# Attention plus mixture-of-experts layer: ranks product behind the up product of its step, slots of the table of pairs 64 bytes apart

## The reference

```python
x = x + attention(layernorm(x))      # 8 heads of 16, causal, 2048 keys a sequence
xt = layernorm(x)
scores = sigmoid(xt @ gate_w.T)                       # 8 experts
top_scores, top_idx = top_k(scores, 2)
top_scores = top_scores / (sum(top_scores) + 1e-20) * 2.5
h, u = xt @ w1[e], xt @ w3[e]                         # 512 -> 352, for each expert e
routed = sum over the two experts of (silu(h) * u) @ w2[e] * score
shared = silu(xt @ sw1) * (xt @ sw3) @ sw2
x = x + routed + shared
```

## Time and profile before

| | |
|---|---|
| median of 3 runs | 1486.96 us |
| the profiled execution, its own time | 1488.37 us |
| its span, first to last instruction | 1486.5 us |
| mean granted TensorE clock, share of 2.4 GHz | 0.969 |
| PE, DVE, ACT, POOL busy | 93%, 64%, 60%, 30% of the span |

### The profile page before, as it was taken

How to read it: one execution, slowest core, us unless ns; L and a number is a source line. 1 busy time by engine, 2 the same in 40 slices (tenths; PEclk the granted TensorE clock), 3 DMA queues, 4 the chain that set the end, 5 groups by cost and what they waited for, 6 DMA issues and landing times.

```text
span 1486.5 us, 22931 instructions
## 1 busy us (share of the span) xinstructions
PE 1377.3 (93%) x5750; PEld 671.1 (45%) x5751; DVE 951.4 (64%) x2758; ACT 890.7 (60%) x2587; POOL 452.0 (30%) x431
## 2 busy tenths in 40 slices
PE   6997999999999999899899977599999999999996
PEld 4553233333333332355455543255555555555553
DVE  3898998888888874588879885333344444444331
ACT  4663456766666777556555645266666666666663
POOL 0000000000000000000112243677777777777771
PEclk9997899999999999999999998799999999999998
DMA  7775410040050000256577763144444344433442
GB/s 219 231 218 161 109 40 5 24 96 5 9 125 5 1 5 12 84 179 204 144 191 176 211 130 78 45 72 74 74 73 73 71 73 71 73 71 71 71 73 34
DMA packets 124858, 136.83 MB, mean 92 GB/s; under 512 B 37046, under 2 KB 86590, under 8 KB 124774
## 3 DMA queue, kind: packets, MB, share of 16 engines
q1 hardware_dynamic: 101350, 96.56, 24.5%
q0 software_dynamic: 21520, 37.84, 13.8%
q10 hardware_dynamic: 1904, 1.46, 0.4%
HBM read 87.03 MB, written 48.83 MB: 91 GB/s over the span
## 4 chain that ended last, share of the span: by engine, by line
PE 73%; DVE 14%; issue 5%; DMA 4%; ACT 3%; SPq 1%; ACTq 0%; POOL 0%; DVEq 0%; POOLq 0%
PE psum L1052 28%; PE psum L1063 15%; PE psum L975 9%; PE psum L957 7%; PE psum L939 6%; PE psum L889 4%; DVE arena L1242 3%; DVE psum L1240 2%; DMA xn_rows<-xg 1%; DMA attn_cur<-attn_rows 1%; DVE stats L1123 1%; PE psum L960 1%; PE psum L1036 1%; ACT arena L723 1%; PE psum L882 1%
## 5 line engine op out<-in xcount | busy, mean ns | idle before, releaser
L1052 PE MATMUL psum<-arena,xg_t 128*128 (+2 forms) x1648 | 515.5, 466 | 18.9 <-DVE xg_t L1212 18.9
L824 ACT COPY act_t<-act_q 32x96 f32<-32x96 f32 x1648 | 431.8, 262 | 153.2 <-DVE act_q L1333 132.6
L1052 PEld LDWEIGHTS psum<-arena,xg_t 128*128 128x128 f32 x1648 | 315.2, 193 | 220.1 <-issue 63.9
L795 ACT ACTIVATE arena<-psum 128x512 f32<-128x512 f32 (+3 forms) x640 | 303.1, 536 | 172.1 <-PE psum L960 84.6
L657 POOL DMA_INDIRECT table<-const,slot_i x64 | 63.0, 984 | 845.1 <-DVE slot_i L1435 748.6
L673 POOL DMA_INDIRECT xq<-xn_rows,quad_rows x284 | 271.5, 956 | 94.2 <-issue 86.6
L1063 PE MATMUL psum<-arena,act_t 128*128 (+3 forms) x618 | 285.7, 598 | 6.2 <-ACT act_t L824 6.2
L1242 DVE TENSOR_REDUCE arena<-psum 128x1 f32<-128x512 f32 x384 | 251.5, 685 | 41.4 <-PE psum L939 40.8
L939 PE MATMUL psum<-arena 96*128 96x512 bf16 (+3 forms) x640 | 219.5, 363 | 17.2 <-DVE arena L1240 9.2
L957 PE MATMUL psum<-arena 99*128 99x512 bf16 (+3 forms) x640 | 215.0, 353 | 1.6 <-ACT arena L795 0.4
L1323 DVE TENSOR_TENSOR act_sb<-psum,silu 128x352 f32<-128x352 f32 x103 | 53.9, 523 | 238.8 <-ACT silu L847 238.2
(11 more groups left out here) (137 smaller groups left out, 843.3 us busy)
## 6 DMA issues: line engine op xcount, KB each, us to landing
arena<-qk_parts SPq DMA_DIRECT2D x48, 256.0 KB, 6.0
arena<-in_w SPq DMA_DIRECT2D x16, 704.0 KB
arena<-in_x SPq DMA_DIRECT2D x32, 256.0 KB, 4.3
x<-in_x SPq DMA_DIRECT2D x32, 256.0 KB, 3.5
xn_rows<-xg SPq DMA_DIRECT2D x32, 256.0 KB, 2.6
xq<-xn_rows SPq DMA_DIRECT2D x128, 64.0 KB, 2.9
out_rows<-y_sb SPq DMA_DIRECT2D x32, 256.0 KB, 3.3
qk_parts<-arena SPq DMA_DIRECT2D x16, 384.0 KB, 3.2
```

Of the source, the lines that this page charges most:

```text
L795: nc.scalar.activation(probs[:, at_b % PS, d * P:], psum[:, NA + at_b % NBK, 0:CH - d * P], ACT.Exp, scale=float(HD) ** -0.5).then_inc(s_e, 1)
L824: i = nc.scalar.copy(dst, src)
L1052: i = nc.tensor.matmul(psum[:, bank + k % 2, 0:w], xg_t[:, k % 2, c, :], rhs, start=c == 0, stop=c == DC - 1)
```

## The change

- PE: in a step of `COUNT_AT`, `ranks(g)` stands behind `up(n)` instead of at the start of the step. `front(n + 2)` and `turn(n + 3)` go ahead of it, so `ranks` waits for one transposed tile more (`n + 4`) and the wait for `s_cntr` moves to the `turn` of the next step (`n - 4 in COUNT_AT`).
- DVE: `slots(g)` stands behind `turn(n + 1)` of the step instead of at its start.
- The table has 16 words (64 bytes) a slot instead of 2; a put still writes 8 bytes, at slot number times 8 in a view of 8-byte elements, for which `slot_i` is made by a multiplication instead of a copy. The load of a block's pairs takes 256 bytes a partition instead of 32, and the row numbers read every sixteenth word.
- The fill of the table, now 2.16 MB instead of 0.27 MB, moves in SP's queue from the third projection chunk to behind the last load of the second unit's keys and values, in the attention.
- `iota_be` (71 x 8 words a partition) becomes `iota_b` (71 words) and is broadcast over the experts; the constants that are loaded first shrink from 845 to 348 words a partition.

In the diff the first `step` is PE's, the second DVE's.

```diff
+PAIR = 16
...
-               ("quarter", 1), ("own", QP), ("pairs", 2 * TOP_K * NT), ("spare_pairs", 2 * P)):
+               ("quarter", 1), ("own", QP), ("pairs", 2 * TOP_K * NT), ("spare_pairs", PAIR * P)):
...
-        table = dram("table", [TABLE, 2])
+        table = dram("table", [TABLE, PAIR])
...
-                if n == 2:
-                    spare = io["const"][:, CONST["spare_pairs"][0]:CONST["spare_pairs"][1]]
...
                     if n < 2:
                         load_unit(1, (n,))
+                    if n == 1:
+                        spare = io["const"][:, CONST["spare_pairs"][0]:CONST["spare_pairs"][1]]
+                        blocks_of = table.rearrange("(b r) a -> b (r a)", r=P)
+                        for b in range(0, TABLE // P, P):
+                            m = min(P, TABLE // P - b)
+                            sp.dma_start(blocks_of[b:b + m, :], spare[0:m, :]).then_inc(s_table, 16)
...
-                            out=table[:, :], out_offset=bass.IndirectOffsetOnAxis(ap=slot_i[:, q, tt:tt + 1], axis=0),
+                            out=table.rearrange("r (s a) -> (r s) a", a=2), out_offset=bass.IndirectOffsetOnAxis(ap=slot_i[:, q, tt:tt + 1], axis=0),
...
-                    if n - 3 in COUNT_AT:
-                        pe.wait_ge(s_cntr, COUNT_AT[n - 3] + 1)
+                    if n - 4 in COUNT_AT:
+                        pe.wait_ge(s_cntr, COUNT_AT[n - 4] + 1)
...
                 def step(n, k):
-                    if shared and n in COUNT_AT:
-                        ranks(COUNT_AT[n], min(n + 3, NT))
                     if shared and k < count - 2:
                         front(n + 2, k + 2)
                     if shared and k < count - 3:
                         turn(n + 3, k + 3)
                     up(n, k, expert(n))
+                    if shared and n in COUNT_AT:
+                        ranks(COUNT_AT[n], min(n + 4, NT))
                     if k >= 1:
                         down(n - 1, k - 1, expert(n - 1))
...
                 def step(n, k):
-                    if shared and n in COUNT_AT:
-                        slots(COUNT_AT[n])
...
                         if k < count - 1:
                             turn(n + 1, k + 1)
+                        if n in COUNT_AT:
+                            slots(COUNT_AT[n])
...
-                    i = nc.vector.tensor_copy(slot_i[:, q, t0:t0 + m], pick[:, 0:m])
+                    i = nc.vector.tensor_scalar(slot_i[:, q, t0:t0 + m], pick[:, 0:m], float(PAIR // 2), None, ALU.mult)
```

More of the change, by code:

```diff
@@ L48 @@
 QW = P // QP
+PAIR = 16
 CONST = {}
 _at = 0
-for _n, _w in (("ident", P), ("rev8", E), ("first_slot", E), ("iota_be", NB * E),
-               ("quarter", 1), ("own", QP), ("pairs", 2 * TOP_K * NT), ("spare_pairs", 2 * P)):
+for _n, _w in (("ident", P), ("rev8", E), ("first_slot", E), ("iota_b", NB),
+               ("quarter", 1), ("own", QP), ("pairs", 2 * TOP_K * NT), ("spare_pairs", PAIR * P)):
     CONST[_n] = (_at, _at + _w)
@@ L71, in constants @@
     put("first_slot", (np.arange(E) * T)[None])
-    put("iota_be", np.repeat(np.arange(NB), E)[None])
+    put("iota_b", np.arange(NB)[None])
     put("quarter", np.arange(P)[:, None] // QW)
@@ L77, in constants @@
     put("pairs", pairs.reshape(P, -1))
-    spare = np.zeros((P, P, 2), np.float32)
+    spare = np.zeros((P, P, PAIR), np.float32)
     spare[:, :, 0] = T + np.arange(P)[None]
@@ L335, in program @@
         NQ = 4
-        block_quads = sb("block_quads", [P, NQ, 2 * QP])
+        block_quads = sb("block_quads", [P, NQ, PAIR * QP])
         quad_rows = sb("quad_rows", [P, NQ, QP], i32)
@@ L1309, in row_numbers @@
                         dve.wait_ge(ss[f"rows_{k % 2}"], QP * (used(n - NQ, k - NQ) + 16))
-                    quad = block_quads[:, k % NQ, :].rearrange("p (g a) -> p a g", a=2)
+                    quad = block_quads[:, k % NQ, :].rearrange("p (g a) -> p a g", a=PAIR)[:, 0:2, :]
                     own = cf("own").rearrange("p (a g) -> p a g", a=1).broadcast_to([P, 2, QP])
@@ L1449, in block_list @@
                 chain(nc.vector.tensor_tensor_scan(ends, blocks, zero, 0.0, ALU.add, ALU.add))
-                chain(nc.vector.tensor_tensor(by_block, over_b(ends), cf("iota_be").rearrange("p (b e) -> p b e", e=E), ALU.is_le))
+                chain(nc.vector.tensor_tensor(by_block, over_b(ends), cf("iota_b").rearrange("p (b a) -> p b a", a=1).broadcast_to([P, NB, E]), ALU.is_le))
                 chain(nc.vector.tensor_reduce(eid, by_block, AX.X, ALU.add))
@@ L1456, in block_list @@
                 chain(nc.vector.scalar_tensor_tensor(block_slot, eid, float(T // P), start, ALU.mult, ALU.subtract))
-                chain(nc.vector.tensor_tensor(block_slot[0:1, :], block_slot[0:1, :], cf("iota_be")[0:1, :].rearrange("p (b e) -> p b e", e=E)[:, :, 0], ALU.add))
+                chain(nc.vector.tensor_tensor(block_slot[0:1, :], block_slot[0:1, :], cf("iota_b")[0:1, :], ALU.add))
                 chain(nc.vector.tensor_scalar(start_i[:, :], block_slot[0:1, :], float(QW), None, ALU.mult))
```

## The result

| | before | after |
|---|---|---|
| median of the runs, us | 1489.08 (1484.05 to 1494.01, 4 runs) | 1467.3 (1465.11 to 1468.95, 4 runs) |
| the profiled execution: own time, span | 1488.37, 1486.5 | 1468.95, 1467.1 |
| TensorE's mean granted clock | 0.969 | 0.969 |

The ratio is 0.984, with a 95% interval from 0.9814 to 0.9866: faster by 1.6%, forecast 1468.5. (Ratios and intervals here are those on record; they are not the quotients of the medians beside them, from which they differ by up to 0.002.) The total came out as forecast, but not for the reasons given: most of the gain hangs on the spacing, which the forecast had put at 2.4 us.

A forecast was written before the change was run, and what follows sets the result against it. PE was taken as the bound, busy nearly throughout, with DVE nearly as long. Terms -6.5 - 1.1 - 7.8 - 0.7 - 2.4 = -18.5 us, from the median 1486.96, gave 1468.5 us; range for 8 in 10: 1460 to 1481.

The forecast's parts named there:

- Groups 2 to 5 and the seam: Step 27 to first routed product: PE stops waiting for `carry`, group 5's ranks run earlier; -7.8 us (-8.5 to -4.5).
- One sign: Expected in the changed profile: no PE wait for the read of the ranks, and `carry` waits over 0.5 us only at group 5.
- Cured: If spacing stops the clogging: tile 15 in time -1.1, `turn(31)` -1.9, last put -1.0; together -4.0 us.
- Groups 0 and 1: Steps 12 to 15: tile 14 ahead of the puts, -6.5 us (-7.7 to -3); step 20: `front(22)` earlier, -1.1 (-1.6 to 0).
- the walk: Following each group along DVE through the shared expert, counting no PE wait as gained by itself; `up(14)` at 740.9, `up(15)` at 749.3.
- The spacing: Slots 64 bytes apart let row stores land faster beside the puts: -2.4 us, between -4.0 if cured and 0 if not.
- Spacing does nothing: Rival: writes stay 8 bytes, so wider slots change nothing; -16.1 us, 1470.9 us; chance 0.25.
- The store and reload stay the bound: Rival: puts still meet tiles 14, 15 and 29, DVE waits for reloads in PE's place; 1479 us, chance 0.20.
- Slower: wider slots clog more: Rival: wider slots and regions make puts hold up HBM longer, stores over 8 us in the median; 1505 us, chance 0.05.
- Constants, -0.7: Kernel start: smaller constants load sooner, PE's first matmul at 9.6 to 10 us; -0.7 us (-1.0 to 0).
- The fill, 0: Attention, from about 168 us: filling the larger table takes 9 to 17 us of DMA engines with little else to do; 0 us.
- The rest of the kernel: From the first routed product to the end: unchanged at 540.5 us.

## Why the prediction was right in its total and wrong in its parts

*Groups 2 to 5 and the seam, -7.8: right.* The second stretch of the table is 7.5 us shorter with the order, under either spacing. One sign was not met: no wait for the read of the ranks was to be left, and at group 2 there is one of 2.06 us. Cured, the forecast has 1.9 for `turn(31)` and 1.0 for the last put on top, -10.7 in all; measured -9.9. `turn(31)` stands in DVE's order of time right behind the product, without a wait, where it was 1.95 us late:

```profile
890.10 0.53 DVE L1324 TENSOR_TENSOR act_sb<-psum,silu 128x352 f32<-128x352 f32 x1 [5.36 <-ACT silu L848]
...
891.16 0.67 DVE L1213 STREAM_TRANSPOSE xg_t<-xq 128x512 f32<-128x512 f32 x1
```

*Groups 0 and 1, -6.5 and -1.1 without a cure: wrong, and this is the step that failed.* It said of tile 15 that "its store at 739 meets the puts, and I allow 1.1 us for that". The store met six puts in a burst and took 8.2 us; DVE waited 6.80 us for the reload (5.7 of them unallowed) and PE 8.47 for the attention tile. The forecast had seen that the slots come some 6 us later, but took the puts to follow at two a step, and did not look at the thresholds that release them. Measured for the two groups: +4 to +9, not -7.6. With 64 bytes, where a burst does no harm, the walk holds: `up(14)` at 740.13 (forecast 740.9), `up(15)` at 748.57 (forecast 749.3), and the stretch of both groups 10.2 us shorter against 8.7 forecast with tile 15 in time.

*The spacing, -2.4, bounds -4.0 and 0: mis-sized.* That neighbouring slots slow the stores was right, and the landings fell to 2.1 us, as for the cured case; the line of 64 bytes was not. But the spacing is worth 13 to 14 us with the old order and 19 with the new. The reason given for the half weight, that slow landings come with neighbouring slots only, stood in no row: the kernel before has no other slots to compare with. The error was to price it as what it adds to a walk that was right already. The walk itself assumed stores of 2.2 us, and of the waits of the kernel before that came from slow landings (4.64 on DVE, 5.00 on PE) it gave the whole to the order. With the spacing and the old order both are gone, and `up(15)` starts at 747.35. Since the cured walk was right and the order and the spacing only wrongly divided, the sum stood: 22.8 forecast at its end, 18.5 taken, 21.8 measured (1489.08 - 1467.3). That 1468.5 came within 1.2 us of the measured time is in part luck: the gain was 3.3 us larger than forecast, but the forecast counted from a median of 1486.96, and with the fourth run it is 1489.08. It is luck too that the whole change was forecast: for the order alone the same terms gave 1473 us, and it took 1489.9.

*The rivals.* "Spacing does nothing" was to give 1470.9; the kernel that is just that (8 bytes, all else changed) takes 1486.5. The Trainium skill, DMA: Bandwidth & Descriptors, Specifications, says that a DMA engine does a read-modify-write below 512 B. Every put here writes 8 bytes, however far apart the slots, and 8 and 32 bytes apart differ by 19 us (1486.53 and 1467.43); so that rule alone does not foretell what counts here. "The store and reload stay the bound" describes the order alone in kind: the waits moved to the reloads and the attention tiles. But it was priced at 1479 and measured at 1489.9: it too left out the burst. "Slower: wider slots clog more" is refuted at both ends: the landings fell, and 512 KB between regions cost nothing (1467.7). The same page of the Trainium skill, in the table with the HBM row pitch, names slower copies at powers of two from 512 KiB on; of these only 512 KiB, as the distance of the regions, was tried here, and it shows no loss.

*Constants, -0.7:* the first matmul came at 9.75 (forecast 9.6 to 10), yet `up(7)` only 0.4 us earlier, and alone they cannot be measured. *The fill, 0:* right, and right in its old place too. *The rest of the kernel:* from the first routed product to the end 541.7 us, where 540.5 was forecast.

What stays open: why the distance counts, of the slots and of the regions. Of the regions it could be where in memory the eight runs of slots fall, or how many writes to one place are under way at once; no run here tells them apart.

## What to carry to other kernels

Where many small writes go out beside larger transfers, first look at how long the same transfer takes with and without them, and treat that as a term of its own: a walk that silently assumes the fast landing credits its gain to whatever else is changed. When work that releases writes is moved later, look at their thresholds too: what was spread may now go in one burst. A few bytes of padding between the targets (32 were enough here) can be worth more than the reordering beside it, and make the reordering pay.

## What the runs showed of the hardware

POOL's writes of 8 bytes to slots 8 bytes apart (regions 32 KB apart) slowed SP's stores of 256 KB from 2.2 us to between 3.1 and 4.4 us in the median, over five kernels. A store among six puts of 128 writes each took 8.2 us, and the next one, behind two puts more, 9.3. At 16 bytes apart the median was 2.2 again, at the same size of write; at 64 bytes a store among six puts took 2.1. I had expected a limit at a 64-byte line, if any.

A long wait costs PE twice. After 8.47 us of waiting, in the kernel with the order alone, the granted clock was 0.50 from 757 to 762 us, the lower of its two levels (1.2 GHz), and the next product took 7.77 us, not 4.95:

```profile
757.48 0.48 PE L1028 MATMUL psum<-const,attn_cur 128*128 128x128 f32 x1 [8.47 <-DMA attn_cur<-attn_rows]
757.75 7.77 PE L1052 MATMUL psum<-arena,xg_t 128*128 128x360 f32 x16
...
757.00:762.00 5.00, 4.52 (x9) 2.68 (x10) 2.99 (x15) 0.27 (x1) 0.00 (x0) 0.50 0.39 110
```
